# Spare bf16 products of constants on TensorE where it waits, in a two-layer Perceiver kernel

## The reference

```python
x = x + _L0_xattn_ref(_layernorm(x, axis=-1), ctx_1024, mask_Bx1xSxS2_ff0, ...)
x = x + _L0_attn_ref(_layernorm(x, axis=-1), ...)
x = x + _L0_ffn_ref(_layernorm(x, axis=-1), ...)
x = x + _L1_xattn_ref(_layernorm(x, axis=-1), ctx_1024, ctx_1024, ...)
x = x + _L1_attn_ref(_layernorm(x, axis=-1), ...)
x = x + _L1_ffn_ref(_layernorm(x, axis=-1), ...)
```

## Time and profile before

| What | Value |
|---|---|
| Median of 3 runs | 333.61 us (333.51 to 333.70) |
| The profiled execution | 331.68 us |
| Its span, first to last instruction | 329.7 us |
| Mean granted TensorE clock in it | 0.928 |
| Busy: PE | 285.2 us (87%) |
| Busy: DVE | 231.8 us (70%) |
| Busy: ACT | 206.7 us (63%) |
| Busy: POOL | 71.5 us (22%) |
| Chain that ended last, by engine | PE 69%, DVE 14%, issue 8% |

### The profile page before, as it was taken

One profiled execution on the slowest core, in us unless ns is written; L12 is line 12 of the kernel. 1 busy time (PEld: TensorE's weight loads), 2 busy tenths in 40 slices (PEclk: granted clock), 3 DMA queues, 4 the chain that ended last, 5 costly groups with the idle time before them and its releaser, 6 DMA issues.

```text
span 329.7 us, 10086 instructions
## 1 busy us (share of the span) xinstructions
PE 285.2 (87%) x4246; PEld 186.9 (57%) x4246; DVE 231.8 (70%) x374; ACT 206.7 (63%) x423; POOL 71.5 (22%) x136
## 2 busy tenths in 40 slices
PE   7847999999999997889648899999999984894886
PEld 5334566667676644735315566767666653342655
DVE  5935899999999835363556899999999803714572
ACT  4572698988989872324402698988989870251141
POOL 5792500000000025220360630000000000300033
PEclk9996999999999998799965999999999995899599
DMA  7943325522224505220000025422231000000000
GB/s 256 414 158 116 126 74 203 174 76 79 72 88 126 213 2 191 95 89 12 0 0 0 2 75 175 165 75 84 66 90 60 3 2 0 2 2 0 0 2 16
DMA packets 10688, 27.84 MB, mean 84 GB/s; under 512 B 2209, under 2 KB 3169, under 8 KB 10258
## 3 DMA queue, kind: packets, MB, share of 16 engines
q1 hardware_dynamic: 10568, 26.97, 24.4%
q10 hardware_dynamic: 74, 0.20, 0.2%
HBM read 20.74 MB, written 6.42 MB: 82 GB/s over the span
## 4 chain that ended last, share of the span: by engine, by line
PE 69%; DVE 14%; issue 8%; ACT 3%; DMA 3%; POOL 2%; SPq 1%; DVEq 0%; POOLq 0%
PE bank L932 67%; DVE mx L698 4%; DVE s_neg L767 1%; DMA k_scratch<-kparts 1%; DMA kpair<-k_scratch 1%; DVE kparts L668 1%; POOL y L324 1%; DVE xn L656 1%; DVE k_rest L665 1%; PE bank L1152 1%; PE bank L963 1%; ACT probs L470 0%; ACT xnT L423 0%; DVE v_all L758 0%; SPq L236 0%
## 5 line engine op out<-in xcount | busy, mean ns | idle before, releaser
L698 DVE TENSOR_REDUCE mx<-bank 128x2 f32<-128x1024 f32 x128 | 154.4, 1224 | 21.7 <-PE bank L932 18.0
L470 ACT ACTIVATE probs<-bank 128x512 f32<-128x512 f32 x256 | 139.4, 595 | 18.2 <-PE bank L932 14.0
L932 PE MATMUL bank<-q_exp,kpair 64*128 64x128 bf16 x1024 | 84.9, 217 | 1.3 <-ACT probs L470 0.5
L932 PE MATMUL bank<-kpair,q_rows 64*128 64x512 bf16 x256 | 74.6, 394 | 8.6 <-DMA kpair<-k_scratch 7.1
L932 PE MATMUL bank<-probs,v_all 128*9 128x128 f32 x2048 | 79.9, 274 | 1.1 <-ACT probs L470 1.0
L932 PEld LDWEIGHTS bank<-q_exp,kpair 64*128 64x128 bf16 x1024 | 55.7, 94 | 31.6 <-issue 15.0
L932 PEld LDWEIGHTS bank<-probs,v_all 128*9 128x9 f32 x2048 | 43.2, 90 | 15.3 <-ACT probs L470 4.0
L361 POOL CAST m_rows<-negm 128x2 bf16<-128x2 f32 x32 | 6.2, 193 | 154.4 <-DVE negm L705 154.4
L932 PEld LDWEIGHTS bank<-kpair,q_rows 64*128 64x128 bf16 x256 | 22.7, 94 | 10.4 <-issue 7.8
L423 ACT ACTIVATE v_all<-bank 128x512 f32<-128x512 f32 (+1 forms) x18 | 10.1, 575 | 23.8 <-PE bank L932 23.8
L324 POOL TENSOR_TENSOR y<-ve,mhalf 128x2 f32<-128x2 f32 x6 | 4.2, 695 | 54.1 <-DVE ve L647 54.1
(11 more groups left out here) (209 smaller groups left out, 348.9 us busy)
## 6 DMA issues: line engine op xcount, KB each, us to landing
k_scratch<-kparts SPq DMA_DIRECT2D x24, 256.0 KB, 2.9
kpair<-k_scratch SPq DMA_DIRECT2D x63, 96.0 KB
kpair<-k_scratch SPq DMA_DIRECT2D x63, 64.0 KB
ctxT_s<-in_ctxT SPq DMA_DIRECT2D x4, 512.0 KB, 6.6
mask_s<-in_mask SPq DMA_DIRECT2D x2, 1024.0 KB, 10.7
kpair<-k_scratch SPq DMA_DIRECT2D x63, 32.0 KB
wM<-in_packM SPq DMA_DIRECT2D x1, 1728.0 KB, 7.1
wB<-in_packB SPq DMA_DIRECT2D x1, 727.0 KB, 6.4
```

What stands on the lines that cost most here:

```text
L470: act.activation(probs[:, j % 4, :], bank[:, 4 + j % 2, :], ACT.Exp).then_inc(S("exp_done"), 1)
L698: V.tensor_reduce(mx[n % 2][:, w, :], bank[:, 2 * (w % 2):2 * (w % 2) + 2, :], AX.X, ALU.max) \
L932: return T.matmul(out_, lhsT=lhsT, rhs=rhs, start=start, stop=stop, **kw)
```

## The change

A helper `keep_clock(o, n)` on PE issues n products of `ident_b` with 512 columns of `selq`, both constants, into bank o; nobody reads them. They wait for nothing and signal nobody. They are placed ahead of waits of PE: in `transpose_xn` with counts from the table `KEEP_NORM`, whose pairs are bank and count (n0, n1 and n2: none; n3: 8; n4 and n5: 12), before the wait for the query rows at the start of `cross(l)` (6 in layer 0, 4 in layer 1), at the start of `cross_out(l)` (4) and before the wait for `oT` in layer 1 (3), around the last transposes of `self_attention(1)` (8 and 3), and before the wait for `q_split` of layer 1 (9). Nothing is removed, and no other instruction moves.

```diff
--- before.py
+++ after.py
@@ -34,6 +34,7 @@
 VP = 32
 Q_BANK = (0, 1, 4, 5)
 WARM = 36
+KEEP_NORM = dict(n0=(7, 0), n1=(5, 0), n2=(5, 0), n3=(5, 8), n4=(5, 12), n5=(7, 12))
 EARLY_BANK = ((2, 3, 6, 7), (2, 3, 2, 3))
 V_BANK = ((2, 3, 6, 4, 5, 7, 4, 5), (7, 6, 7, 6, 4, 5, 7, 4))
 V_EARLY = (3, 4)
@@ -931,6 +932,11 @@
             def mm(out_, lhsT, rhs, start=True, stop=True, **kw):
                 return T.matmul(out_, lhsT=lhsT, rhs=rhs, start=start, stop=stop, **kw)
 
+            def keep_clock(o, n):
+
+                for _ in range(n):
+                    mm(bank[:, o, :], ident_b[:, :], selq[:, 0:512])
+
             def prep_k(l, c):
                 if l == 0:
                     pe.wait_ge(S(f"in_ctx{c // 2}"), 16)
@@ -958,6 +964,7 @@
                 last.then_inc(S("v_proj"), 1)
 
             def transpose_xn(ph):
+                keep_clock(*KEEP_NORM[ph])
                 for b in range(B):
                     pe.wait_ge(S(f"{ph}_xn"), b + 1)
                     last = T.transpose(bank[:, 0, b * P:(b + 1) * P], xn[:, b, :], ident)
@@ -1047,6 +1054,7 @@
                         .then_inc(S("o_heads"), 1)
 
                 k1_at = {(14, 3): 0, (15, 0): 1, (15, 1): 2, (15, 2): 3}
+                keep_clock(7, 4 if l else 6)
                 pe.wait_ge(S("q_rows"), 2 * (l + 1))
                 pe.wait_ge(S("q_rows2"), 2 * (l + 1))
                 for i, (n, w) in enumerate([(0, 0), (0, 1), (0, 2), (0, 3), (1, 0), (1, 1)]):
@@ -1083,6 +1091,7 @@
                 heads(NN - 1)
 
             def cross_out(l):
+                keep_clock(5, 4)
                 pe.wait_ge(S("o_div"), B * (l + 1))
                 pe.wait_ge(S("max_done"), 4 * NN * (l + 1))
                 if l == 0:
@@ -1097,6 +1106,8 @@
                     mm(bank[:, 4, 0:P], C_("w_dq"), C_("w_uqT"))
                     mm(bank[:, 4, P:2 * P], C_("w_uqT"), C_("w_dq"))
                     mm(bank[0:64, 4, 2 * P:3 * P], B_("w_uv", 64), B_("w_oT")).then_inc(S("fold1"), 1)
+                else:
+                    keep_clock(5, 3)
                 pe.wait_ge(S("oT"), l + 1)
                 for b in range(B):
                     last = mm(bank[:, 1 + b, 0:P], oT[:, b * P:(b + 1) * P], WO[l])
@@ -1207,10 +1218,12 @@
                 for b in range(B):
                     back(b)
                 if l:
+                    keep_clock(7, 8)
                     pe.wait_ge(S("att"), 4)
                     for b in range(B):
                         last = T.transpose(bank[:, 3, b * P:(b + 1) * P], att[:, b, :], ident)
                     last.then_inc(S("attT_p"), 1)
+                    keep_clock(7, 3)
                     pe.wait_ge(S("attT"), 1)
                     for b in range(B):
                         last = mm(bank[:, 4, b * P:(b + 1) * P], attT[:, b * P:(b + 1) * P], B_("aoT"))
@@ -1271,6 +1284,7 @@
                 early_k(1, i)
             norm("n3")
             query(1)
+            keep_clock(5, 9)
             pe.wait_ge(S("q_split"), 2)
             pe.wait_ge(S("v_copied"), 8 + 4)
             pe.wait_ge(S("k_staged"), 4 + 4)
```

## The result

| | before | after |
|---|---|---|
| median, four runs each | 333.56 us (332.0 to 333.7) | 328.04 us (327.75 to 330.34) |
| profiled execution | 331.68 us | 328.21 us |
| its span, mean granted clock | 329.7 us, 0.928 | 326.2 us, 0.974 |

The account below looks back on a forecast made before the run. Chain of waits runs through PE, whose clock falls to 0.50 in five places, 47.8 us together. Terms 0 + 2.0 + 1.5 + 1.9 - 0.7 = 4.7 us; 333.61 - 4.7 = 328.9, range 326.8 to 333.3 (forecast's own 327.5 to 330.5).

Parts of the forecast that it names:

- the end: After `comb`: PE idles over 4 us waiting, the clock falls and the end runs partly slow, taken as -1.3 us.
- first scores: Layer 0: six products, 1.3 us, sit at the start of PE's 7.10 us wait for the keys' DMA; gain 0.
- end of cross 0, n1: Four products fill PE's 0.87 us wait for the division, so `prep_v` runs at high clock: +2.0 us, bounds 0 to 2.5.
- n3, query, first scores of layer 1: Products in three waits speed the second transpose, query, `place_q` and first scores: +1.5 us taken, 3.3 if the clock holds.
- end of cross 1, n4: Output products, transposes, query, keys and scores run at high clock: +1.9 us, bounds +1.0 and +2.1.
- last division, n5 up to `comb`: Late products cost 0.2 and 0.1 us; transposes and router's products at high clock give +0.9 until DVE's routing chain starts.
- The price of a product: Each spare product on PE, 512 columns over 128 rows, costs 0.21 us at high clock and 0.43 at low.
- the slower rival: Products run at low clock in front of waiting work, at `q_split`, `oT`, n4 and n5: +4.7 us, 338.3; chance 0.12.
- The second case of the text: n3 to layer 1: clock falls behind the query, nine slow products restore it before `place_q`; gain 3.3 - 1.65 = 1.65 us.
- six to seven: Sign in layer 1: six to seven us instead of 8.7 from first score to `negm`.
- the first case: n3 to layer 1: the clock stays high throughout, gaining 3.3 us.
- What the prediction quotes on transposes: Skill page: transposes don't count as busy for the clock, so n3's two don't hold it; sum then nears first rival's 331.4.

## Why the prediction was right, and where it was not

The forecast of 328.9 us stands against 328.04, and faster was the likeliest sign. The mechanism holds: spare products in the gaps keep the clock up where it fell, and the gain comes from what lies right behind. The closeness of the total is partly luck: three stages won 7.3 us where 5.4 were forecast, and the start and the end lost 4.5 us where 1.3 were. By the traces the parts were:

| part | predicted | trace against trace |
|---|---|---|
| first scores | 0 | -1.4 |
| end of cross 0, n1 | +2.0 | +2.8 |
| n3, query, first scores of layer 1 | +1.5 | +2.6 |
| end of cross 1, n4 | +1.9 | +1.95 |
| last division, n5 up to `comb` | +0.6 | +0.74 |
| the end | -1.3 | -3.1 |

**The price of a product** was right: 0.21 at high clock, 0.43 at low, against 0.23 (twelve in 2.75 us) and 0.42 (nine in 3.79 us). No group at high clock with a record of each product exceeded the 0.27 at which the slower rival would have decided.

**First scores.** The step that failed is "right at the start of that wait, with over 4 us idle behind them; the DMA hides them". They come out of the branch 6 us later and cost 2.24 us ahead of the scores; the kernel without the branch shows the cause. I had read the 7.10 us of the earlier trace rows as one wait with one releaser, when it is two laid over each other: the profile names the one that came last. A loss lay outside the bounds of 0 to +0.9 altogether. How large it is depends on what one counts from. The first `negm` of after is 1.4 us later than in the one trace of before; in the seven traces with these six behind the branch it comes at 36.2 us on average (34.9 to 37.4), in the four without (before among them) at 36.0 (34.7 to 37.3). These times mix in when the branch ended, which was anywhere from 25.87 to 28.08. Counted from there, the seven take 9.6 us on average to the first `negm` (9.0 to 10.3) and the four 8.85 (8.7 to 9.2). So the six cost about 0.8 us here. Trace against trace it is 1.0 us from the branch's end on, and 0.4 us because the branch of after ended later. Three of the four without them take 0.3 to 0.4 us more in cross 0, which gives part of it back.

**End of cross 0.** It won 2.8 us where the upper bound was 2.5: I took 2.0 of 2.36 in case the clock fell later in the stretch; it didn't fall. Without the four products the loss is back at its place, and larger (10.46 us for the stage against 9.30 in before).

**n3 to layer 1.** The second case of the text came true to the letter: the clock fell behind the query, the nine products were slow, `place_q` came at 171.09 though `q_parts` was ready about 1.0 us sooner, and the clock was back before it. From first score to `negm` it took 6.26 us, in the "six to seven" that were named. I had set the lateness at 1.65, and it was 1.0, which is over half of the difference between 1.5 and 2.6. Where the clock didn't fall at n3 at all (three traces, 12.7 us), the stage wins 3.6, near the 3.3 of the first case. What the prediction quotes on transposes stays untested: no run here separates them from other work.

**End of cross 1, n4.** 1.95 for 1.9; taking the products away lost 2.08 in the stage.

**The end.** The mechanism was named, and its size was missed. The step that failed is "a low stretch of length L does L/2 of work that takes L/1.6 at high clock and costs 0.375 L: 1.3 us for 3.55". The wait for `comb` was 2.90 us instead of over 4 (the prediction's own rows give 3.2: 314.95 less 308.38 + 3.4), the low stretch came (6.83 us from 310.73), and it cost 3.1 us instead of 1.3. Two things were too small. L was taken as 3.55 us and was 6.83, which by the formula 0.375 L gives 2.6 us. And the formula assumed that PE is idle for two tenths of the stretch, from the slices, where the window shows it busy for 6.83 of 6.83 us: without slack the price goes towards half of L, 3.4 us. The whole part, from the last division on, came to 0.74 - 3.12 = -2.4 us, half a microsecond beyond its bound of -1.9. This is the term that made the change worth some 2.5 to 3 us less than it could have been, by the ratios: the kernels that either fill the wait or leave the inner products slow both get it back.

**What stays open.** A slow end goes with the wait: in all six traces with 2.90 us of it the end takes 15.0 to 15.9 us, in the three that fill it and in which the clock held it takes 12.1, in the four where the inner products were slow enough to leave 1.47 us or less (before, and the kernels without the products of n3, of cross 1, and of n5) it takes 11.9. But why the clock fell among the inner products without n3's or cross 1's products, and not in after, no run isolates; nor why it fell early in cross 1 in two traces and in self-attention 1 in one. Part of the gap between 5.5 us by medians and 3.5 by traces is that the trace of before is of a short execution. After, run again, gives 4.7 us by medians and 4.4 by its ratio, on eleven runs of before and six of after, which are the better numbers for the gain.

## What to carry to other kernels

Where the granted clock falls after short idle gaps, fill the gap just before work on the critical path, with no more products than fit at the high clock's price, and look next at the waits that the now faster engine creates: a gain that ends in an idle wait can be paid back with interest right behind it. Work that was slow but ended just in time cost nothing, and speeding it up is the one edit to leave out. A wait that the profile puts down to one releaser may hide a second one, such as a branch; what is placed "into" it lands only behind the last that comes before it in program order.

## What the runs showed of the hardware

- Products of constants whose result nobody reads keep the clock up as other products do: four of them in 0.8 us turned 129.51 to 136.34 from 0.50 to 1.00, and without them it was 0.50 again from 129.61 to 139.85. Six that ended 4.9 us ahead of the next work did not keep it up (it fell at 26.97).
- A branch on a loaded register holds PE's instruction stream for 3.49 to 5.21 us at this place (thirteen traces), and PE counts as idle in it unless products were queued ahead: 22 of them ran from 21.65 to 26.56, while the branch's record ran from 23.40.
- The clock can stay low although PE is busy without a gap: 17.07 us at 0.50 in self-attention 1, in one execution, through `mask_s` and `k_s` products on 32 rows among others. A busy figure alone doesn't tell that the clock will rise.
- The length of one wait went with the state of the clock behind it: 2.90 us of idle PE at `comb` came with 6.8 to 10.2 us at 0.50 in six traces of six, beginning in the wait or up to 2.3 us behind it; 0.2 to 1.5 us of idle had none behind them in four of four.
